# Gated delta stage: the triangular mask of the decays, a second product on TensorE or a factor in VectorE's flush

## What is computed

```python
def step(state, inp):
    q_t, k_t, v_t, g_t, b_t = inp
    state = state * jnp.exp(g_t)[:, :, None, None]
    kv_mem = jnp.einsum('bhd,bhde->bhe', k_t, state)
    delta = (v_t - kv_mem) * b_t[:, :, None]
    state = state + jnp.einsum('bhd,bhe->bhde', k_t, delta)
    out_t = jnp.einsum('bhd,bhde->bhe', q_t, state)
    return (state, out_t)
```

## Time and profile before

| what | us |
|---|---|
| median of 3 runs | 4380.82 |
| lowest and highest run | 4380.45, 4384.73 |
| the profiled execution, own time | 4387.09 |
| the profiled execution, span | 4385.2 |
| DVE `flush` in the profile, first and last start | 1620.6, 4016.6 |
| instructions in the profile | 71563 |

### The profile page before, as it was taken

How to read it: one execution, slowest core, us unless ns; L and a number is a source line. 1 busy time by engine, 2 the same in 40 slices (tenths; PEclk the granted TensorE clock), 3 DMA queues, 4 the chain that set the end, 5 groups by cost and what they waited for, 6 DMA issues and landing times. The chain is left out here.

```text
span 4385.2 us, 71563 instructions
## 1 busy us (share of the span) xinstructions
PE 3694.7 (84%) x23438; PEld 2308.9 (53%) x23438; DVE 2976.6 (68%) x7155; ACT 2211.1 (50%) x5604; POOL 2000.9 (46%) x4629
## 2 busy tenths in 40 slices
PE   3569999999589257999999999999999999998486
PEld 2332332332355135666666666666666666666343
DVE  5348888884332445777877877778778778776513
ACT  2435666667013034565565565556565555664210
POOL 0000000000020327777777777777777777787100
PEclk7768999999589668999999999999999999999798
DMA  0000000000052101111111111111111111111000
GB/s 29 0 0 1 1 1 1 1 1 2 17 190 87 57 27 26 36 27 33 32 26 36 36 36 26 36 34 22 35 36 36 26 36 36 27 29 24 8 25 19
DMA packets 258539, 127.21 MB, mean 29 GB/s; under 512 B 218770, under 2 KB 241171, under 8 KB 257300
## 3 DMA queue, kind: packets, MB, share of 16 engines
q1 hardware_dynamic: 255124, 114.50, 10.3%
q0 software_dynamic: 3072, 8.39, 0.6%
HBM read 87.22 MB, written 35.39 MB: 28 GB/s over the span
## 5 line engine op out<-in xcount | busy, mean ns | idle before, releaser
L1686 POOL TENSOR_TENSOR dl_blocks_tmp<-dl_blocks_l,dl_blocks_x 128x60 f32<-128x60 f32 (+24 forms) x1984 | 723.9, 365 | 333.4 <-DMA dl_blocks_l<-lm_dram 192.7
L1691 POOL TENSOR_TENSOR dl_blocks_x<-dl_blocks_x,dl_blocks_tmp 128x60 f32<-128x60 f32 (+24 forms) x1984 | 704.2, 355 | 155.5
L550 DVE TENSOR_REDUCE part_max<-mx 128x1 f32<-128x512 f32 x1024 | 636.8, 683 | 80.4 <-PE mx L412 80.3
L486 ACT ACTIVATE normed_t<-sc 128x1024 f32<-128x1024 f32 x512 | 496.4, 1021 | 221.2 <-PE sc L423 220.9
L1855 DVE SCALAR_TENSOR_TENSOR dl_conv<-dl_raw,dl_weights,dl_conv 128x512 f32<-128x512 f32 x768 | 571.8, 772 | 16.3 <-ACT dl_conv L1619 9.7
L1409 PE MATMUL prep<-normed_t,dl_weights 128*128 128x512 f32 x1024 | 486.8, 599 | 18.4 <-DMA dl_weights<-in_w_delta 16.6
L412 PE MATMUL mx<-k_t,q_t 96*128 96x512 bf16 x1024 | 374.1, 400 | 11.1 <-DVE part_max L550 9.2
L1618 ACT ACTIVATE dl_raw<-prep 128x512 f32<-128x512 f32 x256 | 152.9, 597 | 437.8 <-PE prep L1409 437.8
L395 POOL COPY v_staged<-v 128x256 f32<-128x256 f32 x16 | 6.3, 400 | 703.4 <-PE o_ps L435 703.4
L1758 DVE SCALAR_TENSOR_TENSOR dl_r<-rec_a,t_neg_decay,dl_v_scaled 128x128 f32<-128x128 f32 x512 | 156.0, 346 | 249.4 <-PE rec_a L1478 247.3
L1568 ACT ACTIVATE dl_q_state<-rec_a,t_neg_decay 128x128 f32<-128x128 f32 x512 | 159.6, 364 | 298.5 <-DVE dl_r L1758 298.5
(11 more groups left out here) (279 smaller groups left out, 7950.2 us busy)
## 6 DMA issues: line engine op xcount, KB each, us to landing
dl_blocks_l<-lm_dram SPq DMA_DIRECT2D x256, 128.0 KB, 2.7
dl_weights<-in_w_delta SPq DMA_DIRECT2D x16, 776.0 KB, 4.4
lm_dram<-dl_lm SPq DMA_DIRECT2D x256, 32.0 KB, 1.7
xs_dram<-dl_blocks_x SPq DMA_DIRECT2D x256, 32.0 KB, 2.0
dl_inverse_t<-xs_dram SPq DMA_DIRECT2D x256, 32.0 KB, 2.2
rows_dram<-moe_y_rows SPq DMA_DIRECT2D x1, 6016.0 KB, 22.3
moe_x_rows<-rows_dram SPq DMA_DIRECT2D x47, 128.0 KB, 2.2
back_dram<-moe_y_rows SPq DMA_DIRECT2D x47, 128.0 KB, 1.7
```

The source lines that it names most:

```text
L486: act.activation(probs[:, e % 2, u * 2 * BQ:(u + 1) * 2 * BQ], flat(sc[u][:, :, :]), ACT.Exp, scale=float(DH) ** -0.5).then_inc(s["exp_don ...
L550: dve.reduce_max(part_max[:, t % NT, x[2]:x[2] + 1], bank_of(x)[:, :], AX.X).then_inc(s["ring_read"], 1)
L1686: pool.tensor_tensor(out, L[:, 0:i, i].unsqueeze(1).broadcast_to([P, NM - c0, i]), Xs[:, c0:NM, i:i + 1].broadcast_to([P, NM - c0, i]), AL ...
L1691: pool.tensor_tensor(Xs[:, c0:NM, 0:i], Xs[:, c0:NM, 0:i], out, ALU.add).then_inc(s["solve_step"], 1)
```

## The change

The second product of `decays` goes, and with it the table `neg` (one memset and one select on POOL, whose count of steps falls from 14 to 12). `flush` becomes one scalar_tensor_tensor: max(x, 1e-18), then times the mask `upto`, read with a broadcast over the four matrices of the group. Where the mask is one the value is now max(x, 1e-18) without the subtraction; where it is zero the exponent is a sum over no element, Exp gives one, and the product gives zero. Nothing else changes.

```diff
--- before.py
+++ after.py
@@ -1098,7 +1098,6 @@
 
             for name in ("upto", "after", "ones"):
                 linked(pool.memset(tab[name], 1.0))
-            linked(pool.memset(tab["neg"], -30000.0))
             linked(pool.memset(tab["half"], 0.5))
             linked(pool.memset(tab["mhalf"], -0.5))
             linked(pool.memset(flat(tab["unit"]), 0.0))
@@ -1106,7 +1105,6 @@
                 out=ap, in_=ap, compare_op=op, fill=0.0, base=base, pattern=pattern, channel_multiplier=mult))
             sel(tab["upto"], [[1, P]], 0, -1, ALU.is_ge)
             sel(tab["after"], [[-1, P]], 0, 1, ALU.is_gt)
-            sel(tab["neg"], [[-1, P]], 0, 1, ALU.is_gt)
             for cq in range(4):
 
                 rows = tab["unit"][BLK * cq:BLK * (cq + 1), :, :]
@@ -1121,7 +1119,7 @@
                     last = pe.matmul(ab[t // 8][:, t % 8, :], c.XT[:, k, t * P:(t + 1) * P], W[:, k, :],
                                      start=(k == 0), stop=(k == KD - 1))
             last.then_inc(s["ab_done"], 1)
-            pe.wait_ge(s["masks_done"], 14)
+            pe.wait_ge(s["masks_done"], 12)
             pe.wait_ge(s["gate_link"], 7)
             for i, m in enumerate(("upto", "after", "ones")):
                 last = pe.matmul(flat(sums[i][:, :, :]), tab[m], flat(tab["g"]), start=True, stop=True)
@@ -1185,7 +1183,6 @@
         for name in ("upto", "after", "ones"):
             tab[name] = f(name, [P, P])[:, :]
         tab["norm_w"] = f("norm_w", [P, 1])[:, :]
-        tab["neg"] = f("neg", [P, P], BF16)[:, :]
         tab["half"] = f("half", [P, QC])[:, :]
         tab["mhalf"] = f("mhalf", [P, VH])[:, :]
         tab["unit"] = f("unit", [P, NM, BLK])[:, :, :]
@@ -1369,9 +1366,8 @@
                 else:
                     pe.wait_ge(s["keys_done"], 4 * p + 2)
                 bank = PB[2 if g == 0 else 0]
-                pe.matmul(flat(bank[:, :, :]), tab["after"], flat(gu[:, GM * g:GM * g + GM, :]), start=True, stop=False)
-                pe.matmul(bank[:, :, :], c.identb[:, :], tab["neg"].unsqueeze(1).broadcast_to([P, GM, P]),
-                          start=False, stop=True).then_inc(s["d_mm"], 1)
+                pe.matmul(flat(bank[:, :, :]), tab["after"], flat(gu[:, GM * g:GM * g + GM, :]), start=True, stop=True
+                          ).then_inc(s["d_mm"], 1)
 
             def turn_v(n, p, i):
                 pe.wait_ge(s["silu_done"], 4 * p + 4)
@@ -1815,8 +1811,9 @@
 
             def flush(p, g):
                 dve.wait_ge(s["exp_done"], 2 * p + g + 1)
-                part = flat(attn_[p % DEPTH][:, GM * g:GM * g + GM, :])
-                dve.tensor_scalar(part, part, TINY, TINY, ALU.max, ALU.subtract).then_inc(s["flushed"], 1)
+                part = attn_[p % DEPTH][:, GM * g:GM * g + GM, :]
+                kept = tab["upto"].unsqueeze(1).broadcast_to([P, GM, P])
+                dve.scalar_tensor_tensor(part, part, TINY, kept, ALU.max, ALU.mult).then_inc(s["flushed"], 1)
 
             def scale_v(p, i):
                 dve.wait_ge(s["tv_mm"], 2 * p + i + 1)
```

## The result

The changed kernel takes 4403.9 us, median of five runs (4397.1 to 4413.9); the kernel before, run beside it, 4382.8 (4380.5 to 4387.6). The ratio is 1.0049, interval 1.0033 to 1.0065: slower, by 21 us where 10 were forecast, and inside the stated range. The profiled execution took 4405.8 us, its span 4403.8 against 4385.2. From the first to the last end of `flush_blocks` there are 63 periods; they took 2413.2 us after and 2397.6 before, 15.6 more. What lies ahead of the first took 2.4 us more, what lies behind the last 0.6.

A forecast was written before the change was run, and what follows sets the result against it. The prediction took the ring of GpSimd and SP to bound the kernel: +0.52 us for GpSimd's hold less 0.35 given back, +0.17 us a period times 60, gave 4391 us, range 4367 to 4415 us.

The forecast's parts named there:

- The ring: GpSimd, SP, GpSimd: 7.26 us moving blocks plus 30.71 us of GpSimd make the whole 37.97 us period; no TensorE product in it.
- the fourth rival: TensorE is the bound after all: 64 x 0.52 = 33 us go, 4348 us; chance 0.06.
- TensorE's lead: Two products fewer put TensorE up to 0.52 us a period ahead; its solved-blocks wait grows from 0.95 to about 1.5 us.
- VectorE's flush, +0.33 us each: Each flush goes from 421 ns to the convolution's 752, 0.66 us a period, of which 0.62 goes into idle time.
- the cover: Idle time behind VectorE's flushes: the residual waited 0.35 us for TensorE, the corrections 0.27, taking 0.62 of the 0.66.
- GpSimd beside the flush, +0.52: GpSimd's solve rows held up by VectorE's new flush: 0.26 us each, +0.52 a period, between 0 and 0.66.
- What TensorE's lead gives back, -0.35: Earlier convolutions fall more into GpSimd's 7.26 us with little to do: -0.35 us a period, between 0 and -0.75.
- 0.75 us for a shift of 0.77: Two turns compared: convolutions ending 0.77 us earlier against GpSimd's rows went with 0.75 us less GpSimd time; half was taken.
- The clock, charged at nothing: TensorE's longer waits were taken not to lower its granted clock of 1.00, the full 2.4 GHz: no charge.
- The sum: +0.52 - 0.35 = +0.17 us a period, times 60 = +10 us, on the median 4380.8: 4391 us.
- The first rival: TensorE's lead gives nothing back: the ring pays 0.52 to 0.66 us a period, 4412 to 4420 us; chance 0.22.

The follow-up runs named there:

- a row out of GpSimd: The kernel before with row 1 of the solve left out (two GpSimd instructions per turn, not computed): 4350.7 us, ratio 0.9926.
- the product twice: The kernel before with the mask's product issued twice on TensorE, old flush kept: 4383.0 us, ratio 0.9998.
- the two single runs: Kernel before with the new flush alone, both products kept: 4414.5 us; changed kernel with the old flush, second product out, mask left out: 4375.0 us.

## Why the prediction was right in its sign and low in its size

- **The ring sets the period**: right, for 57 of the 64 turns. The moves of the turn shown are the same 7.26 us, SP issues 0.03 us behind GpSimd, a row out of GpSimd gives 32 us. TensorE's bound, the fourth rival, falls with the product twice, which costs nothing.
- **TensorE's lead ends in its wait for the solved blocks**: right: 0.95 to 1.61 us.
- **VectorE's flush, +0.33 us each**: mis-sized, 684 ns and not near 750, so +0.26 each. The residual behind the first flush shows no wait any more (2456.01, right behind 2455.26 + 0.69), where it had 0.35 us: the cover was there, as was said.
- **GpSimd beside the flush, +0.52**: right, between its ends of 0 and 0.66: 0.57. The Trainium skill (SBUF — State Buffer, Who interferes with whom) says that a VectorE instruction with two SBUF inputs and a GpSimd instruction that reads SBUF exclude each other, and that the later one waits for the first to finish. The trace agrees twice: the rows beside the flush end just after it, and with one of its inputs in PSUM nothing is held. Charging the whole extra duration, as the prediction did by the letter, gives with the measured one 2 x 0.263 = 0.53 us, as good as the term taken.
- **What TensorE's lead gives back, -0.35**: this is the step that failed, in the words "0.75 us for a shift of 0.77", halved. It made 21 us of the lead; taken out alone the product gave 8, put in twice it cost none. Two things were wrong in it. The convolutions don't move by the whole lead: 0.25 us of 0.52. And the slope of the two turns doesn't hold: between the kernels, over 54 turns each, it is 0.06 / 0.25 = 0.2 us of GpSimd for each us with the product out, and 0.10 / 0.63 = 0.2 in the changed kernel, where the longer ring moves them 0.63 us. So the convolutions gave back 0.10 us a turn there, where 0.35 was taken.
- **The clock, charged at nothing**: a term that was missed. Its ground, waits of 2.1 us "in a stage that holds the clock at 1.00", rests on the one period of the earlier trace rows; in the same trace the clock fell in two turns, after waits of 1.90 and 2.59 us. With the longer waits it fell in seven, and SP's lateness in such turns went from 7.5 to 13.0 us.
- **The sum**: with the two single runs it would have been 32 - 8 = 24 us in place of 10; 21 were measured. The first rival, no give-back at all, was 31 to 40: the truth lies between it and the forecast. That it stayed that far below the rival is in part luck: the moves, which the prediction held fixed, became 10.4 us shorter in all.
- **Not foreseen**: the flush of the blocks lengthened by 75 ns (1142 to 1217), as it now meets more of VectorE's gates: where it meets them it took 1242 ns (1149 before), where it doesn't 1084 (1083 before). This is 5 of the 21 us; that it is the gates was read from the timelines, not tested.

## What to carry to other kernels

Where GpSimd stands in the ring that sets the period, an edit on VectorE is priced by what it holds of GpSimd, and that hangs on where its inputs lie: a longer instruction that reads PSUM was cheaper here than a short one that reads SBUF. A slope that is to carry a forecast is read over all turns of the trace, not from two. And what is taken out of a ring is worth its length only until the next way round, here SP's queue behind VectorE, is as long. And a lead that ends in a longer wait isn't free because the wait is idle: look, over all turns, at the clock that TensorE is granted behind such waits.

## What the runs showed of the hardware that was not expected

The 128x512 flush took 684 ns as a scalar_tensor_tensor with an immediate and two SBUF inputs, 752 as the convolution, whose scalar is read from a table. The old tensor_scalar took 421 ns from SBUF to SBUF and 690 from PSUM to SBUF; beside the first GpSimd's rows lost 0.17 us each time, beside the second nothing. So VectorE's faster form from SBUF is also one that holds GpSimd, and its slower form from PSUM freed the engine that counted.
